# A four-layer modulated 1-D convolution: the second quad's seven-tap filter composed in one step on TensorE ahead of the loop, and GpSimd's clears and one bias addition put elsewhere

## The reference

```
def _layer(x, style, w, b, mw, mb, typ):
    s = style @ mw.T + mb
    weight = SCALE * w * s[:, None, :, None]
    demod = lax.rsqrt(jnp.sum(weight * weight, axis=(2, 3)) + EPS)
    weight = weight * demod[:, :, None, None]
    if typ == 'same':
        out = jax.vmap(_conv_same)(x, weight) + b[None, :, None]
    elif typ == 'upsample':
        out = jax.vmap(_conv_up)(x, weight.transpose(0, 2, 1, 3)) + b[None, :, None]
        out = _blur(out, 2.0 * blur_k, (1, 1))
    elif typ == 'downsample':
        xb = _blur(x, blur_k, (2, 2))
        out = jax.vmap(_conv_down)(xb, weight) + b[None, :, None]
...
x = x + _L0_cond_ref(x, cond_512, weights, biases, mod_w, mod_b)
```

## Time and profile before

| | before |
|---|---|
| median of 3 runs | 157.92 us (156.2 to 158.38) |
| the profiled execution, its own time | 156.41 us |
| its span, first to last instruction | 154.5 us |
| PE busy | 143.0 us (93%) |
| VectorE, ScalarE, GpSimd busy | 120.9, 91.8, 85.8 us |
| mean granted TensorE clock | 0.957 |
| DMA | 17.64 MB, mean 114 GB/s |

### The profile page before, as it was taken

How to read it: one execution, slowest core, us unless ns; L and a number is a source line. 1 busy time by engine, 2 the same in 40 slices (tenths; PEclk the granted TensorE clock), 3 DMA queues, 4 the chain that set the end, 5 groups by cost and what they waited for, 6 DMA issues and landing times.

```text
span 154.5 us, 5457 instructions
## 1 busy us (share of the span) xinstructions
PE 143.0 (93%) x2333; PEld 103.3 (67%) x2333; DVE 120.9 (78%) x193; ACT 91.8 (59%) x183; POOL 85.8 (56%) x98
## 2 busy tenths in 40 slices
PE   6789999799999999989998999999999989998950
PEld 5459999576466676647674667687767755776750
DVE  7958797899969997996699668937992899294660
ACT  2516585434465684858675777686767395825540
POOL 7400299299992899999990394059206900970000
PEclk9955699999999999999999999999999999999996
DMA  4983700051000700060798930594064008304626
GB/s 108 318 228 32 272 4 0 4 212 66 0 0 4 271 6 0 4 250 25 160 298 215 275 146 4 116 257 177 4 136 142 4 0 193 83 0 100 180 58 214
DMA packets 9735, 17.64 MB, mean 114 GB/s; under 512 B 4752, under 2 KB 5360, under 8 KB 9712
## 3 DMA queue, kind: packets, MB, share of 16 engines
q1 hardware_dynamic: 9424, 16.98, 38.5%
q10 hardware_dynamic: 288, 0.33, 0.7%
HBM read 8.91 MB, written 8.39 MB: 112 GB/s over the span
## 4 chain that ended last, share of the span: by engine, by line
PE 76%; DVE 12%; ACT 5%; issue 3%; DVEq 0%; ACTq 0%
PE p_c L613 35%; PE p_h L595 12%; PE p_k L557 7%; PE p_k L542 5%; DVE H_sb L1118 3%; PE p_h L475 2%; DVE H_sb L1127 2%; PE p_k L613 2%; PE p_k L572 2%; PE p_h L457 2%; DVE w_sb L1122 1%; DVE w_sb L1106 1%; DVE w_sb L1110 1%; PE p_h L542 1%; PE p_h L723 1%
## 5 line engine op out<-in xcount | busy, mean ns | idle before, releaser
L613 PE MATMUL p_c<-dd_sb,Tw 64*64 64x256 f32 (+1 forms) x544 | 29.3, 363 | 0.2 <-DVE p_c L1178 0.2
L1148 DVE TENSOR_TENSOR p_c<-p_c,s_sb 128x1024 f32<-128x1024 f32 x13 | 16.0, 1233 | 14.3 <-PE p_c L613 10.5
L613 PEld LDWEIGHTS p_c<-dd_sb,Tw 64*64 64x64 f32 x544 | 21.9, 132 | 7.1 <-issue 1.9
L905 ACT ACTIVATE ot<-p_c,pvec 128x508 f32<-128x508 f32 x26 | 20.8, 893 | 8.9 <-PE p_c L613 8.9
L267 POOL TENSOR_TENSOR dx_sb<-xin 128x1032 f32<-128x1032 f32 x8 | 20.6, 2572 | 0.3 <-POOL z_st L308 0.2
L595 PE MATMUL p_h<-H_sb,W_st 64*64 64x448 f32 (+1 forms) x192 | 19.2, 523 | 0.8 <-DVE H_sb L1127 0.8
L247 POOL TENSOR_TENSOR Tw<-Tw,di_sb 128x128 f32<-128x128 f32 x7 | 3.2, 458 | 29.6 <-ACT Tw L867 29.1
L1083 DVE TENSOR_TENSOR d_sb<-xin 128x2072 f32<-128x2072 f32 x8 | 19.5, 2433 | 0.0
L613 PE MATMUL p_c<-dx_sb,Tw 64*64 64x256 f32 x320 | 18.9, 377 | 0.5 <-ACT ot L905 0.5
L1091 DVE TENSOR_TENSOR dd_sb<-d_sb 128x2064 f32<-128x2064 f32 x8 | 19.0, 2375 | 0.1
L613 PE MATMUL p_c<-d_sb,Tw 64*64 64x256 f32 x304 | 18.9, 386 | 0.0
(11 more groups left out here) (184 smaller groups left out, 275.0 us busy)
## 6 DMA issues: line engine op xcount, KB each, us to landing
xin<-in_x_dram SPq DMA_DIRECT2D x16, 512.0 KB, 4.7
out_dram<-ot SPq DMA_DIRECT2D x14, 512.0 KB, 5.7
out_dram<-ot SPq DMA_DIRECT2D x3, 256.0 KB, 3.4
out_dram<-ot ACTq DMA_DIRECT2D x1, 256.0 KB, 4.2
wn<-in_L_cond_weights_dram SPq DMA_DIRECT2D x1, 192.0 KB, 3.6
mwn<-in_L_cond_mod_w_dram SPq DMA_DIRECT2D x1, 128.0 KB, 2.3
xe<-in_x_dram SPq DMA_DIRECT2D x2, 64.0 KB, 10.7
w1n<-in_L_cond_weights_dram ACTq DMA_DIRECT2D x1, 48.0 KB, 2.8
```

The source lines that it names most:

```text
L613: ins = pe.matmul(bank[j * C:(j + 1) * C, i], Tw[q % NW][rows, blk, j, :], moving(rows, j, n), start=(first and n == 0), stop=(n == len(bl ...
L905: act.activation(ot[q % NO_T][:, i, 4 + par:4 + par + 2 * n - 1:2], bank[:, i, 2:2 + n], ACT.Identity, bias=pcol(W_C, 2 * q + i), scale=pc ...
L1148: dve.tensor_tensor(bank[:].rearrange("p i (n h) -> p i n h", h=2), p_a[:, :, w * NQ:(w + 1) * NQ].unsqueeze(3).to_broadcast([P, 2, NQ, 2] ...
```

## The change

The changed kernel makes H of quad 1 with the matmuls of `compose_H` too, and copies it out with `evac_H`; `compose_M`, `evac_M` and the blur on VectorE begin with quad 2. H(1) stands in TensorE's queue behind T(0) and the `zc` matmuls. With that `H_sb` is one buffer instead of two, `yc` goes behind H(0), `yc` and `zc` go to another bank, `product_a2(0)` writes to `p_b` instead of `p_h`, and `compose_T(1)` stands ahead of `product_bc2(0)`, not behind it. On ScalarE the copy `x3` for quad 0 moves behind the one of `o_st`. On VectorE `d_sb` of quad 0 moves behind the sums of quad 0. On GpSimd only `xe` is cleared at the start, `z_st` once the first factors of the demodulation are there, `w_sb` ahead of `dx_sb`, and `x0e`, `ye`, `ze`, `y_st` behind `prod`; the bias addition on `xe` moves from quad 1 of the loop to right behind `xse`.

```
-            for t in (z_st, xe, x0e, ye, ze, y_st, w_sb):
-                pool.memset(t[:], 0.0).then_inc(zeroed, 1)
...
+            pool.memset(xe[:], 0.0).then_inc(zeroed, 1)
             pool.wait_ge(made["a0"], 2)
+            pool.memset(z_st[:], 0.0).then_inc(zeroed, 1)
...
+            pool.memset(w_sb[:], 0.0).then_inc(zeroed, 1)
+            pool.wait_ge(zeroed, 4)
             pool.wait_ge(made["yc"], 1)
             make_dx(pool, 0)
...
+            pool.wait_ge(made["xse"], 2)
+            pool.tensor_tensor(xe[:], xe[:], bias[0:C, 3:4].unsqueeze(1).unsqueeze(1).to_broadcast([C, 2, B, WXE]), ALU.add)\
+                .then_inc(made["xe"], 1)
...
+            for t in (x0e, ye, ze, y_st):
+                pool.memset(t[:], 0.0).then_inc(zeroed, 1)
+            pool.wait_ge(zeroed, 8)
             pool.wait_ge(T_sums, 3)
...
-            compose_H()
-            compose_M(1)
...
             compose_T(0)
...
             ins.then_inc(put["zc"], 1)
+            compose_H(1)
             edge_x0()
...
-                if 0 < q < QUADS - 1:
+                if q + 1 < QUADS:
                     compose_T(q + 1)
                 product_bc2(q)
                 if q == 0:
-                    compose_T(1)
...
-            make_x3(0)
-            evac_H()
-            evac_M(1)
+            evac_H(0)
             act.wait_ge(put["oT"], 1)
             copy(o_st[:], p_y[:, 1, 0:3 * C].rearrange("p (a c) -> p a c", c=C), copied["o_st"], 0.125)
+            make_x3(0)
...
-            make_d(0)
-            blur_begins(1)
             dve.wait_ge(put["zc"], 1)
...
             sum_blocks(dve, 0)
-            blur_ends(1)
+            make_d(0)
             dve.wait_ge(zeroed, 7)
```

More of the change, by code:

```diff
@@ L222, in bank_a2 @@
         def bank_a2(q):
-            return p_b if 0 < q < QUADS - 1 else p_h
-        def bank_M(q):
-            return p_k if q > 1 else p_x
+            return p_b if q + 1 < QUADS else p_h
         def alone(q):
@@ L556, in compose_M, with compose_H @@
                         for j in range(2):
-                            ins = pe.matmul(bank_M(q)[j * C:(j + 1) * C, i, k * C:(k + NR) * C], W1_st[rows, k, :],
+                            ins = pe.matmul(p_k[j * C:(j + 1) * C, i, k * C:(k + NR) * C], W1_st[rows, k, :],
                                             R_sb[q % 2][rows, j], start=(k == 0), stop=(k == K - 1), skip_group_check=True)
                 ins.then_inc(M_done, 1)
-            def compose_H():
-                pe.wait_ge(R_evac, 2)
+            def compose_H(q):
+                pe.wait_ge(R_evac, 2 * (q + 1))
+                if q > 0:
+                    pe.wait_ge(T_evac, 2)
                 for f in range(NF):
@@ L742, in _ @@
             compose_R(1, p_h)
[L743 removed]
+            compose_H(0)
+            pe.wait_ge(copied["W1_st"], 1)
             pe.wait_ge(made["vec"], 1)
             for k in range(K):
[L746 removed]
+                ins = pe.matmul(p_x[0:C, 1, 256:256 + B], wn[:, 1, :, k], vec[0:C, V_B0, 0:B], start=(k == 0),
                                 stop=(k == K - 1))
             ins.then_inc(put["yc"], 1)
[L749 to L751 removed]
+            pe.wait_ge(copied["G_mv"], 1)
             blurred_halves(3, p_y[:, 1], cid1, 3).then_inc(put["oT"], 1)
@@ L754, in _ @@
             pe.wait_ge(made["z_st"], 6)
-            pe.wait_ge(copied["o_st"], 1)
+            pe.wait_ge(made["yc"], 1)
             for k in range(3):
-                ins = pe.matmul(p_y[:, 1, 288:288 + B], z_st[:, k, :], yc[:], start=(k == 0), stop=(k == 2))
+                ins = pe.matmul(p_x[:, 1, 0:B], z_st[:, k, :], yc[:], start=(k == 0), stop=(k == 2))
             ins.then_inc(put["zc"], 1)
+            compose_H(1)
             edge_x0()
             pe.wait_ge(made["zc"], 1)
+            pe.wait_ge(copied["o_st"], 1)
             for k in range(3):
@@ L837, in evac_R @@
                 act.wait_ge(R_done, q + 1)
-                wait(act, H_done, 1 if q > 1 else 0)
-                wait(act, M_done, q - 2)
+                wait(act, M_done, q - 3)
+                if 2 <= q < 4:
+                    act.wait_ge(H_done, q - 1)
                 for j in range(2):
```

98 lines of the change are left out of this document (43 added, 55 removed).

## The result

| | before | changed |
|---|---|---|
| median of the runs taken together | 157.1 us (156.2 to 158.38, 4 runs) | 155.66 us (154.01 to 156.8, 4 runs) |
| measured again, more runs | 156.87 us (35 runs) | 155.66 us (153.4 to 157.42, 12 runs) |
| ratio, 95% interval | | 0.9895 [0.9848, 0.9942], again 0.9854 [0.9814, 0.9895] |
| the profiled execution, its own time | 156.41 us | 156.8 us |
| its span | 154.5 us | 154.6 us |

The account below looks back on a forecast made before the run. TensorE, busy 143.0 of 154.5 us, was taken as the bound. 156.41 + 0.9 - 0.2 - 0.5 = 156.6 us, or 158.1 on the runs' median; the middle, 157.4, was forecast, range 155.6 to 159.8.

Parts of the forecast that it names:

- The clear of `w_sb` ... What is hidden: Prologue and beside TensorE: w_sb's clear (1.05 us) waits for yc anyway; removing quad 1's blur brings nothing by itself.
- the sum: Whole kernel: 156.41 + 0.9 (prologue) - 0.2 - 0.5 (loop) = 156.6 us.
- its half on two SBUF inputs: Port rule: such VectorE instructions contend only with GpSimd instructions reading SBUF, so clears beside VectorE's sums cost nothing.
- My third rival: TensorE's clock falls at idle times near 22.2 and 30.4 us, 5 us lost: 161.6 us; chance 0.03.
- the two footings: The sum on the profiled execution (156.41 us) gave 156.6; on the median of runs (157.92 us), 158.1.
- The prologue: Up to product_a2(0): T(0) starts 1.08 us earlier, product_a2(0) at 30.7, 0.9 us later than before.
- the turns: Prologue: three prod on GpSimd (0.65 us each) alternate with VectorE's identity and three sums, 1.95 us less 0.3 overlap.
- the 157.4 of the forecast: Whole kernel: the forecast time, the middle between 156.6 and 158.1 us.
- The edge chain: Behind the sums, up to edge_y: x0e's copy ends at 39.85, 1.1 us later; edge_y at 40.1, just in time.
- The second rival: GpSimd late for edge_y, x0e's copy ending behind 41.8, TensorE waiting over 2 us: 159.9 us; chance 0.12.
- The first rival: TensorE bound only: prologue costs 0.6 us, all loop waits (0.8 + 0.5) go: 155.7 us; chance 0.2.
- The loop: Quads 1 to 3: 0.2 us gained of the waits for H, 0.5 us wait ahead of R in quad 3 gone.

Follow-up runs that it names:

- x2: Changed kernel with GpSimd's seven clears back at the start, everything else as changed: 156.78 us, ratio to before 0.9993.
- x3: Kernel before with only the clears moved as in the change: 156.58 us, ratio 0.9983.
- x12: Changed kernel with one extra useless matmul in each of two early TensorE pauses and the xe bias addition back in quad 1: 154.18 us, ratio 0.9837.
- x4: Kernel before with three extra useless matmuls filling TensorE's first pause, at 5.44 to 6.37 us: 156.33 us, ratio 0.9984.
- x7: Three extra useless matmuls added to x2: 155.44 us, 0.9924; the same three on the changed kernel (also within "x4 to x7"): 155.62 us, 0.9928.
- x1: Changed kernel measured again without any edit, 12 runs: 155.66 us, ratio 0.9854.
- x11: Changed kernel with one extra useless matmul behind the style transposes and one ahead of R(0): 154.57 us, ratio 0.9865.
- x6: x4 with four more useless matmuls ahead of product_a2(0), so both pauses of the kernel before are filled: 155.22 us, ratio 0.9916.
- x9: Kernel before with only the four extra useless matmuls ahead of product_a2(0): 157.38 us, ratio 1.0037.
- x10: x3 with the four extra useless matmuls ahead of product_a2(0): 156.08 us, ratio 0.9947.
- x8: Changed kernel with the bias addition on xe back in quad 1 of the loop: 155.76 us, ratio 0.9878.

## Why the prediction was wrong, point by point

**The step that failed: "The clear of `w_sb` ... What is hidden", and with it the start of the sum.** I priced the removal of the clears from the start at nothing (only `w_sb`'s clear had a sentence, for its new place) and took everything up to H(0), its clock included, from one execution. The first clears and VectorE's first work stand side by side. VectorE of before, from 3 us to 5 us:

```profile
3.08 2.40 DVE L1003 TENSOR_SCALAR cid<-ident 128x64 f32<-128x64 f32 x3
```

GpSimd of before beside it ends in the clear of `w_sb` at 5.35, and begins with:

```profile
1.82 0.42 POOL L299 MEMSET z_st<- 128x384 f32 x1
...
2.70 0.52 POOL L299 MEMSET x0e<- 128x512 f32 x1
```

The same stretches of the changed kernel, VectorE and then GpSimd:

```profile
3.07 1.21 DVE L1006 TENSOR_SCALAR cid<-ident 128x64 f32<-128x64 f32 x11
```

```profile
1.81 0.57 POOL L294 MEMSET xe<- 64x576 f32 x1
```

Three instructions took 2.40 us before, eleven take 1.21 now; `cid` is done at 4.28 instead of 6.27. It is the clears: with them back (x2) the eleven take 3.21 us again, with them alone moved (x3) 1.21. So a clear does hold up VectorE, if VectorE's instruction is of this kind. The Trainium skill has it in "SBUF — State Buffer", section "SBUF: two separate sides": the lock on the shared port pair is taken by a VectorE instruction in a 2-port mode as well, which `tensor_scalar` can be in, and by any GpSimd instruction. By that rule the trace agrees. I had used only its half on two SBUF inputs, and looked for clears only 20 us further on.

That half held. The changed kernel has two clears beside the last sum, which has its two inputs in SBUF:

```profile
28.43 0.68 DVE L253 TENSOR_TENSOR Tw<-Tw 128x512 f32<-128x512 f32 x1
```

```profile
28.29 0.53 POOL L326 MEMSET x0e<- 128x512 f32 x1
28.75 0.48 POOL L326 MEMSET ye<- 128x448 f32 x1
```

The same sum of before, with GpSimd idle, took as long, and `d_sb` beside the other clears took 2.31 us, as in x2, where they are not there:

```profile
29.67 0.68 DVE L257 TENSOR_TENSOR Tw<-Tw 128x512 f32<-128x512 f32 x1
```

`cid` feeds the blurred taps on TensorE, whose first matmul moved from 6.38 to 5.76. The matmuls of the biases come at 7.03 instead of 7.10, so next to nothing is gained directly in this execution: its TensorE was still at half clock at 5.76 (the first of these matmuls takes 0.79 us, before 0.48), while the clock column says 1.00. In x12, whose clock is full by then, they come at 6.52. But TensorE's idle time of 0.93 us at 5.4 is gone, and x4 to x7 show what that does to the granted clock.

**The clock.** My third rival let the clock only fall. That it could be better than in the one execution of before, and that 10.2 us at half clock are 5 us to be had, I did not ask. In place of nothing, the clears' move is worth 1.1 us in the changed kernel: x2 156.78 us, x1 155.66. Nor did I ask why the profiled execution lay 1.5 us under the median; I bridged the two footings with their middle.

**The prologue, on the slow clock.** There the steps held. x2 has the change's TensorE order and before's clock course: `product_a2(0)` at 29.80. H(0) to T(0) took 4.09 us there, before 4.97: 0.88 saved, forecast 0.8. T(0) to `product_a2(0)` took 7.54, forecast 8.1: 0.6 too long. It was TensorE's own work (forecast 7.8) and not VectorE's sums, as I had it. The bias addition took 1.14, not 1.4, and the turns cost VectorE 1.06 us up to the second sum (0.60, 1.06 and 0.80 us, against 0.29, 0.69 and 0.42 before), not 1.65. VectorE's sums in the changed kernel:

```profile
26.61 1.06 DVE L248 TENSOR_TENSOR Tw<-Tw 128x512 f32<-128x512 f32 x1
27.71 0.80 DVE L251 TENSOR_TENSOR Tw<-Tw 128x256 f32<-128x256 f32 x1
```

and GpSimd beside them:

```profile
24.49 1.14 POOL L317 TENSOR_TENSOR xe<-xe,biases 64x576 f32<-64x576 f32 x1
25.59 2.64 POOL L322 TENSOR_TENSOR prod<-wn,coef 64x256 f32<-64x256 f32 x3
...
30.02 3.51 POOL L331 TENSOR_TENSOR y_st<-y_st,prod 64x256 f32<-64x256 f32 x3
...
37.32 0.55 POOL L354 COPY x0e<-x0e 64x448 f32<-64x448 f32 x1
```

The turns are there as forecast, and the sums are just in time. The two slowest runs of x1, 157.3 and 157.4 us at a mean clock of 0.955, lie 0.5 us above before's at that clock (156.9), where the sum had 0.2. That they are the 157.4 of the forecast is luck: it was the middle of two footings, not a time of either.

**The edge chain.** `x0e` was forecast 9.15 us behind the first product, `edge_y` 9.4; measured 37.87 - 28.61 = 9.26, and `edge_y` at 37.92. The second rival (GpSimd late) did not occur. But GpSimd has no slack left: in x11, whose prologue is faster, TensorE waits 0.26 us for it.

**The first rival's number.** It said 155.7, and 155.66 was measured. That is luck as well: it was to come from a prologue that loses 0.6 us and a loop that wins 1.3, and in the profiles the prologue won 1.2 and the loop 0.5.

**The loop.** Forecast -0.7 us. The mean of the eight profiles with H(1) made directly, from the first product to PE's end, is 118.84 us, that of before, x3, x6, x9 and x10 119.35: -0.5 (x4, with its fall of the clock behind the first product, is left out). By quads it went otherwise. Quad 3 gave 0.95 us instead of 0.5, the 0.5 us wait ahead of R and most of the standing still of line 1118 are gone. Quads 1 and 2 took it back, 0.40 and 0.76 us in this profile and 0.41 and 0.19 in x1's. TensorE of the changed kernel in quad 2,

```profile
66.14 1.21 PE L546 MATMUL p_k<-A_sb,V_st 64*64 64x192 f32 x24 [1.16 <-DVE w_sb L1117]
```

VectorE, and GpSimd ahead of it:

```profile
62.22 3.00 DVE L1113 SCALAR_TENSOR_TENSOR H_sb<-w_sb 128x896 f32<-128x896 f32 x1
```

```profile
61.55 2.31 POOL L263 TENSOR_TENSOR dx_sb<-xin 128x1032 f32<-128x1032 f32 x1
63.81 1.73 POOL L375 TENSOR_TENSOR oe<-oe,xe 64x128 f32<-64x128 f32 x2
```

I had seen that `dx_sb` would collide with this line instead of a later one, and counted a gain of 0.2. The blur instruction now stands behind `dx_sb`, for 3.00 us instead of 1.09, with a turn of `oe` besides. I had not asked what is queued behind `dx_sb`.

**What stays open.** Why the course of the clock differs between executions of the same kernel. The first pause filled, all six profiles (x4 to x7, x11, x12) show R(0) and R(1) near full clock; unfilled, the half clock was long or short. In x3 and x10 it was long without any pause of TensorE between 5 and 14 us. In the changed kernel's runs the late clears make the better course more frequent; what decides it in a single run no experiment here shows. No profile caught one of the changed kernel's runs under 154.4 us, nor one of before at 155.7. The recorded clock column also can't be used to count the courses: see below.

## What to carry to other kernels

In a kernel that TensorE bounds, a change is priced on two courses of its clock: look for idle time of TensorE ahead of a half-clock stretch, in the first microseconds too, and ask what each waiting microsecond gives when the clock is full. A gain may need two places mended at once, the pause that lowers the clock and the next wait that would swallow what the better clock brings; try both together before giving up on either. One useless matmul in such a pause is a cheap experiment, and here a cheap mend.

## What the runs showed of the hardware

- **Clears and `tensor_scalar`.** VectorE's `tensor_scalar` of 128x64 takes about 0.11 us (11 in 1.21); the first three beside a row of GpSimd clears took 2.40 us. Clears beside an addition of two SBUF inputs cost it nothing (0.68 us with and without).
- **Short pauses, long half clocks.** Pauses of 0.6 to 1.7 us were followed by half-clock stretches of 3.4 us (changed, x1, x4, x8) or 10.2 us (before), and in other executions by none (0.64 us ahead of R(0) in x4 and x6). That the pause is the cause rests on x4 to x7, where filling it took the stretch away.
- **The first rise.** The clock also rises at different moments in executions with the same first matmuls. The two at 5 us ran at full clock before, at half clock in the changed kernel:

```profile
5.00 0.44 PE L482 MATMUL p_c<-ident,mwn 128*128 128x128 f32 x2
```

```profile
5.14 0.69 PE L486 MATMUL p_c<-ident,mwn 128*128 128x128 f32 x2
```

The Trainium skill, "TensorE: Matmul & The Clock Gate", Part 1, says of the warm-up that its length varies from one run to the next of the same kernel. The traces agree for kernels that are alike up to there; in x3 and x10 the rise came only at 17 us.
- **The clock's record can miss a stretch.** It says 1.00 for the first microseconds of every profile here, half-clock matmuls or not, and x3's says it up to 40 us. Its window from 10 us, and its R(0):

```profile
10.00:15.00 5.00, 5.00 (x64) 4.56 (x63) 3.62 (x16) 2.42 (x8) 0.00 (x0) 1.00 0.65 107
```

```profile
14.66 2.12 PE L548 MATMUL p_k<-A_sb,V_st 64*64 64x192 f32 x21
```

In x12, 24 such matmuls take 1.21 us. The length of a known group of matmuls is the better witness.
